# The Mamba stage of a kernel of eight sublayers: the input enters by a diagonal matmul, and GpSimd multiplies one half by C in every second step

## The chip, the cores and the metric

One core of one Trainium2 chip runs the kernel. The metric is the device time of one execution in microseconds (us). Times below without another unit are us from the start of the profiled span. VectorE is DVE in the profile, ScalarE is ACT, GpSimd is POOL, TensorE is PE (PEld its weight loads), and the queue of the transfers is SP.

## The reference

Eight sublayers follow one another on x of shape 4 x 1024 x 128 in float32. The change touches only the fifth, a Mamba block with 256 inner channels and 16 states:

```python
xs, z = jnp.split(xn @ W_in.T, 2, axis=-1)
u = jax.nn.silu(conv(xs))                      # depthwise, 4 taps
dt_low, Bc, Cc = jnp.split(u @ W_xproj.T, [DT_RANK, DT_RANK + D_STATE], axis=-1)
delta = jax.nn.softplus(dt_low @ W_dt.T + b_dt)
def step(h, inp):                              # over the 1024 tokens
    dt, bt, ct, ut = inp
    h = jnp.exp(dt[..., None] * A) * h + (dt * ut)[..., None] * bt[:, None, :]
    return h, jnp.einsum('bdn,bn->bd', h, ct)
y = (ys + u * D_param) * jax.nn.silu(z)
return resid + y @ W_out.T
```

## The kernel before

The Mamba stage works in 64 **steps** N, one for each batch b (4) and state n (16): N = 16 b + n. In a step the recurrence over 1024 tokens is one `tensor_tensor_scan` for each half c of the 256 channels: 128 channels lie on the partitions, the tokens along the free dimension. For a step the engines do the following.

- ScalarE, `decay` (L1671): exp(delta * A) of 128x1024 for both halves into `da`. `scale_input` (L1683): eight activations, one for each block of 128 tokens, multiply the block of delta * u (`duT`, tokens on partitions, 256 channels) by the column of B of this state. The result, eight tiles of 128x256, goes to `scaled`, double buffered in the tiles that were called rope, causal and toeplitz.
- TensorE, `drive` (L1544): eight transposes for each half bring `scaled` into PSUM banks 0 to 3 (two banks for each half), channels on partitions. A half's banks are free when its scan of the step before has ended.
- VectorE (L1776): scan of half 0, scan of half 1. Then at most one piece of the layer norm of a later batch, and (L1790) the product of `h` and the row of C, in place, for half 0 and for half 1.
- GpSimd (L1836): for each half, `y_sum` += product. The scan of step N + 2 writes the same buffer of `h` and so waits for this addition of step N.
- SP (L1808): loads the row of C, spread over 128 partitions (512 KB), two buffers. It waits for the products of step N - 2.

Beside the steps of batch b the input of batch q = b + 1 is prepared, one part behind each step, in an order that is written out by hand. TensorE: `convolve` in n = 0, 1, 3, 4; `low_rank` in 5; `gate_input` 0 in 6; `delta` in 7 and 8; `gate_input` 1 in 9; `rates_to_tokens` (B, L1501) in 10; `input_to_tokens` in 12 and 13. All of them use PSUM banks 6 and 7, so that each waits until the part before it is read. ScalarE: `take_convolved` in 2, 3, 5, 6; `activate` (Silu) in 6; `take_low` and `direct` 0 in 7; `take_gate` 0 (Silu, L1641) and `direct` 1 in 8; `take_delta` (L1647, L1649) in 9 and 10; `soften` (Exp, then Ln, L1654 and L1656) in 10; `take_gate` 1 in 11. Silu, Exp and Ln each need a table load of their own when ScalarE changes to them. VectorE copies B from PSUM in step 12 (`take_rates`, L1760); GpSimd computes delta and delta * u in steps 10 and 11 (`step_size`, L1819 and L1822). In steps 2 and 3 the batch before is finished (`results`, L1532).

For batch 0 the same parts run ahead of the first step, on TensorE in the order low, delta, `rates_to_tokens`, gates, `input_to_tokens`. There VectorE copies B only behind the norm of batch 1 (L905) and the last combination of the experts (L768).

Of the kernel before, what the change touches and what calls it, by code (L numbers as in the profile page):

```python
# [1424 lines left out]
def sp_load_stacks(nc, k, sp, sm, b):  # L1425

    for stack, tile in ((k.q_dram[b], k.q_stack[b % 2]), (k.k_dram[b], k.k_stack[b % 2])):
# [5 lines left out]
          "drive", "scan", "prod", "y_sum", "gated", "y_ps", "x_new"]  # L1433
# [12 lines left out]


def pe_mamba(nc, k, pe, sm, moe):

    bank_reader = [None, None]  # L1450

    def take_banks(*halves):
        for g in halves:
            if bank_reader[g]:
                pe.wait_ge(sm[bank_reader[g][0]], bank_reader[g][1])

    def tokens(q):
        take_banks(0, 1)
        for t in range(8):
            if t % 4 == 0:  # L1460
                pe.wait_ge(sm["xn2"], 2 * q + t // 4 + 1)
            mm = nc.tensor.transpose(k.ps[:, PREP + t // 4, (t % 4) * P:(t % 4 + 1) * P], k.XN2s[:, t, :], k.ident[:])
            if t % 4 == 3:
                mm.then_inc(sm["xnT_ps"], 1)
        bank_reader[:] = [("xnT", 2 * q + 1), ("xnT", 2 * q + 2)]

    def convolve(q, c, g):
        take_banks(g)
# [27 lines left out]
    def rates_to_tokens(q):
        take_banks(0)
# [6 lines left out]
        bank_reader[0] = ("bT", q + 1)  # L1504

    def delta(q, c):
        take_banks(0, 1)
        pe.wait_ge(sm["low"], q + 1)
        for g in range(2):
            mm = nc.tensor.matmul(k.ps[:, PREP + g, :], k.WdtT[96:112, c * P:(c + 1) * P], half(k.low[q % 2][96:112, :], g),  # L1510
                                  start=True, stop=True)
        mm.then_inc(sm["delta_ps"], 1)
        bank_reader[:] = [("relu", 2 * q + c + 1)] * 2

    def input_to_tokens(q, r):
        take_banks(0, 1)
        pe.wait_ge(sm["du"], 2 * q + 2)
        for t in range(4 * r, 4 * r + 4):
            g = t % 4 // 2
            for c in range(2):  # L1520
                mm = nc.tensor.transpose(k.ps[:, PREP + g, (t % 2) * 256 + c * P:(t % 2) * 256 + (c + 1) * P],
                                         k.soft[:, c, t * P:(t + 1) * P], k.ident[:])
            if t % 2 == 1:
                mm.then_inc(sm["duT_ps"], 1)
                bank_reader[g] = ("duT", 4 * q + 2 * r + g + 1)

    def results(b):
        take_banks(0, 1)
# [1201 lines left out]
```

## Time and profile before

| what | value |
|---|---|
| three executions | 3139.59, 3144.19, 3144.25 us |
| median of them | 3144.19 us |
| the profiled execution | 3142.85 us, of it the span 3141.1 us |
| first scan, end of the last product | 1901.8 and 2403.9 us: 64 steps in 502.1 us |
| single ScalarE instructions: one half of `decay`; `take_low`; `direct`; one gate; one of `take_delta`'s two; one of `soften`'s two; a table load | 1.14; 1.00; 1.14; 1.02; 1.10; 1.91; 1.28 us |
| the four batches of 16 steps | 132.0, 133.7, 126.6 and 109.8 us |

The profiled execution lies between the runs that were timed and 1.3 us below their median. A row of the timeline gives start, duration, engine, line and operation, and in brackets the idle time of the engine before it and what ended it; neighbours of one kind are merged ("x2"), and the duration is then that of all of them.

### The profile page before, as it was taken

How to read it: one execution, taken by the hardware profiler on the slowest of the kernel's cores; microseconds unless marked ns; L12 is line 12 of the kernel's file. 1: busy time of each engine (PE TensorE's matmuls, PEld its weight loads, DVE VectorE, ACT ScalarE, POOL GpSimd, SP SyncE). 2: the span in 40 equal slices, each digit the busy share in tenths (PEclk: the TensorE clock that was granted, in tenths of full speed). 3: DMA queues.
4: the chain of work that ended last, by engine and by line, in shares of the span. 5: the costliest groups of instructions: out<-in, count | busy, mean ns of one | idle time of the engine just before them, and what ended most of it. 6: DMA issues, size and time to landing. Idle time of an engine off the chain costs nothing.

```text
span 3141.1 us, 55341 instructions
## 1 busy us (share of the span) xinstructions
PE 2592.3 (83%) x19200; PEld 1636.5 (52%) x19200; DVE 2033.0 (65%) x4702; ACT 1779.8 (57%) x3375; POOL 910.1 (29%) x995
## 2 busy tenths in 40 slices
PE   7999799989988998688994856676655988888878
PEld 4667466756665666574444834445443622322325
DVE  5654565456645564557866447898897877777745
ACT  4665466556655665251111438988984446666662
POOL 1000000000000000673005765767776122322221
PEclk9999899989999999699996978677756979999999
DMA  5000000000000000130001311121121530110000
GB/s 178 1 0 1 2 1 0 1 2 1 0 2 1 1 0 25 48 89 20 1 0 36 89 52 47 62 67 62 68 74 63 200 105 2 56 55 2 2 2 28
DMA packets 79895, 113.47 MB, mean 36 GB/s; under 512 B 10109, under 2 KB 48172, under 8 KB 79680
## 3 DMA queue, kind: packets, MB, share of 16 engines
q1 hardware_dynamic: 71488, 97.07, 9.4%
q0 software_dynamic: 8192, 13.67, 1.6%
q8 instruction: 118, 1.93, 0.3%
q14 instruction: 97, 0.79, 0.1%
HBM read 77.66 MB, written 35.78 MB: 36 GB/s over the span
## 4 chain that ended last, share of the span: by engine, by line
PE 21%; POOL 16%; issue 14%; DVE 9%; ACT 1%; POOLq 0%; DVEq 0%; SPq 0%; ACTq 0%
POOL arena L1836 6%; DVE Wqkv L2107 5%; POOL arena L829 4%; PE ps L1983 4%; PE ps L991 3%; POOL slots_in L815 3%; PE ps L1156 3%; PE ps L1955 2%; PE ps L1944 1%; PE ps L1165 1%; PE ps L982 1%; PE ps L1948 1%; PE ps L1992 1%; DVE X L768 1%; PE ps L1191 0%
## 5 line engine op out<-in xcount | busy, mean ns | idle before, releaser
L356 ACT ACTIVATE arena<-ps 128x512 f32<-128x512 f32 (+1 forms) x640 | 334.3, 548 | 309.1 <-PE ps L260 307.7
L432 DVE CUSTOM_DVE_ANT_0 arena<-ps,causal 128x512 f32<-128x512 f32 (+3 forms) x512 | 282.5, 589 | 328.5 <-PE ps L247 328.2
L369 ACT ACTIVATE arena<-arena 128x640 f32<-128x640 f32 (+7 forms) x512 | 394.1, 770 | 36.2 <-DVE arena L432 32.4
L2107 DVE TENSOR_REDUCE Wqkv<-ps 128x2 f32<-128x1024 f32 (+3 forms) x384 | 353.4, 953 | 87.0 <-PE ps L1948 81.7
L2063 ACT ACTIVATE arena<-ps 128x1024 f32<-128x1024 f32 (+3 forms) x384 | 302.4, 809 | 162.3 <-PE ps L1955 158.7
L260 PE MATMUL ps<-ident,arena 128*128 128x128 f32 x2304 | 346.2, 282 | 46.6 <-ACT arena L369 44.6
L1836 POOL TENSOR_TENSOR arena<-arena,W 128x1024 f32<-128x1024 f32 x128 | 333.6, 2626 | 170.4 <-DVE W L1790 170.4
L509 POOL COPY arena<-arena 128x512 f32<-128x512 f32 x64 | 39.5, 617 | 1040.0 <-DVE arena L456 621.4
L260 PEld LDWEIGHTS ps<-ident,arena 128*128 128x128 f32 x2304 | 250.6, 141 | 165.4 <-issue 139.6
L281 PE MATMUL ps<-arena,rope 128*64 128x128 f32 x4608 | 336.3, 281 | 0.0
L1776 DVE TENSOR_TENSOR_SCAN W<-arena,ps 128x1024 f32<-128x1024 f32 x128 | 285.2, 2269 | 56.0 <-ACT arena L1671 45.5
L281 PEld LDWEIGHTS ps<-arena,rope 128*64 128x64 f32 x4608 | 243.6, 136 | 64.3 <-issue 53.5
L247 PE MATMUL ps<-arena 64*128 64x512 bf16 (+3 forms) x2304 | 232.2, 325 | 5.1 <-ACT rope L348 5.1
L1983 PE MATMUL ps<-arena,W 128*32 128x512 f32 (+3 forms) x1536 | 164.4, 500 | 7.2 <-POOL arena L2134 3.6
L1955 PE MATMUL ps<-arena 64*128 64x512 bf16 (+3 forms) x768 | 124.6, 333 | 46.4 <-DVE Wqkv L2107 39.5
L1671 ACT ACTIVATE arena<-arena,A_neg 128x1024 f32<-128x1024 f32 x128 | 142.5, 1141 | 20.1 <-DVE W L1776 19.5
L1790 DVE TENSOR_TENSOR W<-W,select 128x1024 f32<-128x1024 f32 x128 | 153.1, 1237 | 0.5
L1944 PE MATMUL ps<-arena 64*128 64x512 bf16 (+3 forms) x768 | 133.3, 344 | 19.7 <-DVE Wqkv L2107 18.3
L2134 POOL TENSOR_SCALAR_AFFINE_SELECT arena<-arena 128x256 f32<-128x256 f32 x256 | 103.5, 408 | 158.1 <-ACT arena L2063 156.6
L1544 PE MATMUL ps<-ident,rope 128*128 128x128 f32 x512 | 99.0, 362 | 60.8 <-DVE W L1776 55.3
L198 PE MATMUL ps<-XNT,arena 128*128 128x512 f32 x256 | 137.8, 667 | 11.3 <-DVE arena L407 8.6
L247 PEld LDWEIGHTS ps<-arena 64*128 64x128 bf16 x2304 | 88.9, 94 | 109.5 <-issue 50.9
(262 smaller groups left out, 4608.7 us busy)
## 6 DMA issues: line engine op xcount, KB each, us to landing
select<-c_rows SPq DMA_DIRECT2D x64, 512.0 KB, 3.6
arena<-q_dram SPq DMA_DIRECT2D x4, 2048.0 KB, 9.6
arena<-k_dram SPq DMA_DIRECT2D x4, 2048.0 KB, 15.2
q_dram<-arena SPq DMA_DIRECT2D x24, 256.0 KB, 3.7
k_dram<-arena SPq DMA_DIRECT2D x24, 256.0 KB, 3.7
arena<-slots_in SPq DMA_DIRECT2D x8, 640.0 KB, 5.0
slots_out<-arena SPq DMA_DIRECT2D x8, 640.0 KB, 3.8
slots_in<-select SPq DMA_DIRECT2D x4, 640.0 KB, 6.3
```

Source lines behind the costliest of these rows:

```text
L247: mm = nc.tensor.matmul(k.ps[:, banks[h], 0:w], q, kk, start=part == 0, stop=part == 2)
L260: mm = nc.tensor.transpose(k.ps[:, 4 + m % 2, (b - b0) * P:(b - b0 + 1) * P], k.prob[:, n % 2, h, j * P:(j + 1) * P], k.ident[:])
L281: mm = nc.tensor.matmul(k.ps[64 * h:64 * h + 64, 6 + n // 4, (n % 4) * P:(n % 4 + 1) * P], k.v_tok[:, parity, j, 64 * h:64 * h + 64], k.pr ...
L356: nc.scalar.activation(k.probT[:, n % 2, b0 * P:(b0 + nb) * P], k.ps[:, 4 + m % 2, 0:nb * P], ACT.Copy)\
L369: nc.scalar.activation(k.prob[:, i % 2, h, 0:w], k.prob[:, i % 2, h, 0:w], ACT.Exp, bias=k.neg_max[:, i % 2, h:h + 1], scale=-1.0, accum_o ...
L432: ins = nc.vector.tensor_tensor_reduce(k.prob[:, i % 2, h, 512 * g:512 * g + w], k.ps[:, banks[h], 0:w], k.causal[:, first:first + w], 1.0 ...
L1776: nc.vector.tensor_tensor_scan(k.h[:, 2 * (n % 2) + c, :], k.da[:, 2 * (n % 2) + c, :], both(k.ps[:, 2 * c:2 * c + 2, :]), 0.0, ALU.mult, ...
L1836: nc.gpsimd.tensor_tensor(y, y, k.h[:, 2 * (n % 2) + c, :], ALU.add).then_inc(sm["y_sum"], 1)
L1955: mm = nc.tensor.matmul(k.ps[:, 2 * slot + h, 0:w], k.k_stack[b % 2][rows, 2 * Q + a, j * P:(j + 1) * P], k.q_stack[b % 2][rows, 2 * Q + a ...
L1983: mm = nc.tensor.matmul(k.ps[32 * r:32 * r + 32, 6, 512 - w:512], k.v_aug[b % 2][:, j, 4 * Q + r, :], k.expT[:, (2 * s + a) % 4, h, 0:w], ...
L2063: nc.scalar.activation(k.expT[:, n % 4, :, 0:w], k.ps[:, 2 * (m % 3):2 * (m % 3) + 2, 0:w], ACT.Exp, scale=-1.0)\
L2107: nc.vector.tensor_reduce(k.least[:, g, a, i % 4, c, :], k.ps[:, 2 * (m % 3):2 * (m % 3) + 2, 0:search_width(i, c)], AX_X, ALU.min)\
```

## The change

1. `scale_input` no longer scales the data. It multiplies the 128x128 identity by the column of B, eight activations of 128x128 instead of 128x256, into `diag` (two buffers, both in rope). `drive` multiplies: data block (128 tokens x 128 channels, from `duT`) times diagonal, 16 full float32 matmuls in a step in place of 16 transposes.
2. In every odd step the product with C of half 1 is computed on GpSimd, ahead of its two additions. The other three products of two steps stay on VectorE.
3. The preparation uses four PSUM banks (4 to 7), so that parts no longer wait for the reader of the part before; the order is new.
4. For batch 0 the copy of B has a bank of its own (bank 0).

```diff
@@ pe_mamba
-                mm = nc.tensor.matmul(k.ps[:, PREP, t * NSTATE:(t + 1) * NSTATE], k.u[:, c, t * P:(t + 1) * P],
+                mm = nc.tensor.matmul(k.ps[:, at, t * NSTATE:(t + 1) * NSTATE], k.u[:, c, t * P:(t + 1) * P],
...
     def drive(N, c):
+        b = N // NSTATE
         if c == 0:
+            if N % NSTATE == 0:
+                pe.wait_ge(sm["duT"], 4 * b + 4)
             pe.wait_ge(sm["scaled"], 2 * N + 2)
         if N >= 1:
             pe.wait_ge(sm["scan"], 2 * N - 1 + c)
         for t in range(8):
-            mm = nc.tensor.transpose(k.ps[:, 2 * c + t // 4, (t % 4) * P:(t % 4 + 1) * P],
-                                     k.scaled[N % 2][t // 4][:, t % 4, c * P:(c + 1) * P], k.ident[:])
+            mm = nc.tensor.matmul(k.ps[:, 2 * c + t // 4, (t % 4) * P:(t % 4 + 1) * P],
+                                  k.duT[:, 8 * (b % 2) + t, c * P:(c + 1) * P], k.diag[N % 2][:, t, :], start=True, stop=True)
...
-            if n == 5:
+            if n in (5, 6):
+                gate_input(q, n - 5)
+            if n == 7:
                 low_rank(q)
-            if n == 6:
-                gate_input(q, 0)
-            if n in (7, 8):
-                delta(q, n - 7)
-            if n == 9:
-                gate_input(q, 1)
+            if n in (8, 9):
+                delta(q, n - 8)
@@ act_mamba
-            ins = nc.scalar.activation(k.scaled[N % 2][t // 4][:, t % 4, :], k.duT[:, 8 * (b % 2) + t, :], ACT.Identity,
-                                       scale=k.bT[:, at:at + 1])
+            ins = nc.scalar.activation(k.diag[N % 2][:, t, :], k.ident[:], ACT.Identity, scale=k.bT[:, at:at + 1])
...
-            if n == 6:
+            if n == 7:
                 activate(q)
-            if n == 7:
+                take_gate(q, 0)
+                take_gate(q, 1)
+            if n == 8:
                 take_low(q)
                 direct(q, 0)
-            if n == 8:
-                take_gate(q, 0)
-                direct(q, 1)
...
             if n == 11:
-                take_gate(q, 1)
+                direct(q, 1)
@@ dve_mamba
-        for c in range(2):
+        for c in range(1 if shares_product(N) else 2):
             dve.wait_ge(sm["scan"], N * 2 + c + 1)
@@ sp_mamba
-            sp.wait_ge(sm["prod"], 2 * (N - 1))
+            sp.wait_ge(sm["prod"], products_by_dve(N - 2, 1))
+            if shares_product(N):
+                sp.wait_ge(sm["pool_prod"], N // 2)
@@ pool_mamba
+        if shares_product(N):
+            pool.wait_ge(sm["scan"], 2 * N + 2)
+            pool.wait_ge(sm["c_row%d" % (N % 2)], 16 * (N // 2 + 1))
+            h = k.h[:, 2 * (n % 2) + 1, :]
+            nc.gpsimd.tensor_tensor(h, h, k.c_rows[N % 2], ALU.mult).then_inc(sm["pool_prod"], 1)
```

The new helpers: `shares_product(N)` is `N % 2 == 1`; `products_by_dve(N, c)` counts VectorE's products up to step N; `gate_bank(w)` gives bank 6 or 4; `rates_bank(q)` gives bank 0 for batch 0 and 4 for the others. The wait for the last readers of the experts' banks (`yt_act`, `yt_dve`) moves from ahead of the first `drive` to ahead of `rates_to_tokens(0)`.

## Rows read from the trace of the kernel before

**Rows 1.** The page: busy time by engine over the whole span.

```profile
PE 2592.3 (83%) x19200; PEld 1636.5 (52%) x19200; DVE 2033.0 (65%) x4702; ACT 1779.8 (57%) x3375; POOL 910.1 (29%) x995
```

**Rows 2.** Windows per batch: width; PE, PEld, DVE, ACT, POOL busy; clock, DMA share, GB/s.

```profile
1901.80:2033.80 132.00, 86.65 (x378) 61.36 (x377) 119.72 (x117) 123.05 (x202) 95.99 (x37) 0.77 0.18 61
2033.80:2167.50 133.70, 94.95 (x401) 67.05 (x400) 122.18 (x121) 117.22 (x191) 91.04 (x39) 0.72 0.19 64
2167.50:2294.10 126.60, 87.27 (x400) 61.92 (x398) 112.91 (x71) 117.83 (x191) 96.62 (x37) 0.80 0.19 67
2294.10:2403.90 109.80, 57.11 (x272) 46.89 (x272) 109.61 (x69) 76.87 (x140) 78.61 (x33) 0.62 0.21 72
```

**Rows 3.** Waits between 1900 and 2400 us: total, times, longest.

```profile
...
DVE W L1776 <- ACT arena L1671: 45.5, 7, 19.3
...
DVE W L1776 <- issue: 10.5, 6, 3.0
...
```

**Rows 4.** Groups by line and shape, ScalarE: busy us, mean ns of one, idle before.

```profile
L369 ACT ACTIVATE arena<-arena 128x128 f32<-128x128 f32 x64 | 25.7, 401 | 4.1 <-DVE arena L432 4.1
```

**Rows 5.** Timeline before the first scan.

```profile
1882.19 0.29 DVE L1760 COPY arena<-ps 128x128 f32<-128x128 f32 x1
1882.54 3.42 PE L1481 MATMUL ps<-arena,WinT 128*128 128x512 f32 x4 [22.23 <-DVE arena L1760]
...
1895.99 3.30 ACT L1683 ACTIVATE rope<-arena 128x256 f32<-128x256 f32 x8
...
1901.79 4.46 DVE L1776 TENSOR_TENSOR_SCAN W<-arena,ps 128x1024 f32<-128x1024 f32 x2 [19.31 <-ACT arena L1671]
```

**Rows 6.** Timeline of VectorE and of GpSimd, one step of the last batch.

```profile
2383.96 4.45 DVE L1776 TENSOR_TENSOR_SCAN W<-arena,ps 128x1024 f32<-128x1024 f32 x2
2388.34 2.33 DVE L1790 TENSOR_TENSOR W<-W,select 128x1024 f32<-128x1024 f32 x2
2390.59 2.27 DVE L1776 TENSOR_TENSOR_SCAN W<-arena,ps 128x1024 f32<-128x1024 f32 x1
...
2382.98 4.87 POOL L1836 TENSOR_TENSOR arena<-arena,W 128x1024 f32<-128x1024 f32 x2 [1.76 <-DVE W L1790]
2385.86 1.99 POOL L1836 TENSOR_TENSOR arena<-arena,W 128x1024 f32<-128x1024 f32 x1
```

**Rows 7.** Timeline of VectorE and of GpSimd, one step of the third batch.

```profile
2175.45 5.58 POOL L1836 TENSOR_TENSOR arena<-arena,W 128x1024 f32<-128x1024 f32 x2 [4.03 <-DVE W L1790]
...
2180.80 1.32 DVE L1790 TENSOR_TENSOR W<-W,select 128x1024 f32<-128x1024 f32 x1
```

**Rows 8.** Timeline where a product meets a GpSimd instruction.

```profile
2255.61 2.00 POOL L1822 TENSOR_TENSOR W<-arena,W 128x1024 f32<-128x1024 f32 x1
2255.89 2.79 DVE L1790 TENSOR_TENSOR W<-W,select 128x1024 f32<-128x1024 f32 x1
```

**Rows 9.** Timeline of TensorE: eight transposes; results twice (high, lower clock); low_rank.

```profile
2060.43 1.06 PE L1544 MATMUL ps<-ident,rope 128*128 128x128 f32 x8 [0.56 <-DVE W L1776]
...
2056.14 3.74 PE L1532 MATMUL ps<-WoutT,arena 128*128 128x128 f32 x32
...
1948.28 3.66 PE L1491 MATMUL ps<-W,WxT 128*112 128x512 f32 x8 [1.97 <-ACT W L1618]
...
2410.27 5.84 PE L1532 MATMUL ps<-WoutT,arena 128*128 128x128 f32 x32 [13.21 <-DVE arena L1747]
```

**Rows 10.** Timeline of ScalarE, TensorE and VectorE in steps 10 to 12.

```profile
1979.29 1.10 ACT L1647 ACTIVATE W<-ps,s_cols 128x1024 f32<-128x1024 f32 x1
...
1993.13 1.28 ACT L1641 ACT_TABLE_LOAD   x1
...
1988.91 4.46 DVE L1776 TENSOR_TENSOR_SCAN W<-arena,ps 128x1024 f32<-128x1024 f32 x2 [2.25 <-ACT arena L1671]
2004.39 4.46 DVE L1776 TENSOR_TENSOR_SCAN W<-arena,ps 128x1024 f32<-128x1024 f32 x2 [6.06 <-ACT arena L1671]
...
1995.50 4.66 PE L1501 MATMUL ps<-WxT,W 128*128 128x16 f32 x21 [9.94 <-ACT arena L1641]
```

More of the change, by code:

```diff
@@ L1432 @@
           "low_ps", "low", "c_stored", "c_row0", "c_row1", "bT_ps", "bT", "delta_ps", "abs", "relu", "soft", "delta", "du", "duT_ps", "duT", "scaled", "da",
-          "drive", "scan", "prod", "y_sum", "gated", "y_ps", "x_new"]
+          "drive", "scan", "prod", "pool_prod", "y_sum", "gated", "y_ps", "x_new"]
 NSTATE = 16
@@ L1440, in both, with shares_product, products_by_dve, gate_bank @@
     return ap.rearrange("p a b -> p (a b)")
+def shares_product(N):
+    return N % 2 == 1
+def products_by_dve(N, c):
+    return 3 * (N // 2) + (3 if shares_product(N) else c + 1)
 def state_steps(k):
     return [(b, n) for b in range(k.B) for n in range(NSTATE)]
+def gate_bank(w):
+    return (6, 4)[w]
+def rates_bank(q):
+    return 4 if q else 0
 def pe_mamba(nc, k, pe, sm, moe):
[L1450 to L1455, printed above, removed]
+    bank_reader = {bank: None for bank in (4, 5, 6, 7)}
+    def take_banks(*banks):
+        for bank in banks:
+            if bank_reader[bank]:
+                pe.wait_ge(sm[bank_reader[bank][0]], bank_reader[bank][1])
     def tokens(q):
-        take_banks(0, 1)
+        take_banks(6, 7)
         for t in range(8):
@@ L1461, in tokens @@
                 pe.wait_ge(sm["xn2"], 2 * q + t // 4 + 1)
-            mm = nc.tensor.transpose(k.ps[:, PREP + t // 4, (t % 4) * P:(t % 4 + 1) * P], k.XN2s[:, t, :], k.ident[:])
+            mm = nc.tensor.transpose(k.ps[:, 6 + t // 4, (t % 4) * P:(t % 4 + 1) * P], k.XN2s[:, t, :], k.ident[:])
             if t % 4 == 3:
                 mm.then_inc(sm["xnT_ps"], 1)
-        bank_reader[:] = [("xnT", 2 * q + 1), ("xnT", 2 * q + 2)]
+        bank_reader[6], bank_reader[7] = ("xnT", 2 * q + 1), ("xnT", 2 * q + 2)
     def convolve(q, c, g):
-        take_banks(g)
+        bank = 4 + 2 * c + g
+        take_banks(bank)
         if c == 0 and g == 0:
@@ L1490, in low_rank @@
             for g in range(2):
-                mm = nc.tensor.matmul(k.ps[0:112, PREP + g, :], k.WxT[:, c, 0:112], half(k.u[:, c, :], g), start=(c == 0),
+                mm = nc.tensor.matmul(k.ps[0:112, 6 + g, :], k.WxT[:, c, 0:112], half(k.u[:, c, :], g), start=(c == 0),
                                       stop=(c == 1))
         mm.then_inc(sm["low_ps"], 1)
-        bank_reader[:] = [("low", q + 1)] * 2
+        bank_reader[6] = bank_reader[7] = ("low", q + 1)
     def rates_to_tokens(q):
-        take_banks(0)
+        at = rates_bank(q)
+        if q >= 1:
+            take_banks(at)
         pe.wait_ge(sm["u"], q + 1)
@@ L1524, in input_to_tokens @@
                 mm.then_inc(sm["duT_ps"], 1)
-                bank_reader[g] = ("duT", 4 * q + 2 * r + g + 1)
+                bank_reader[bank] = ("duT", 4 * q + t // 2 + 1)
     def results(b):
-        take_banks(0, 1)
+        take_banks(6, 7)
         pe.wait_ge(sm["gated"], 2 * b + 2)
@@ L1640, in take_gate @@
             act.wait_ge(sm["y_ps"], 2 * (q - 1))
-        nc.scalar.activation(k.z[q % 2][:, w, :], both(k.ps[:, PREP:PREP + 2, :]), ACT.Silu).then_inc(sm["z"], 1)
+        at = gate_bank(w)
+        nc.scalar.activation(k.z[q % 2][:, w, :], both(k.ps[:, at:at + 2, :]), ACT.Silu).then_inc(sm["z"], 1)
     def take_delta(q, c):
@@ L1658, in take_input @@
     def take_input(q, r):
+        if q >= 2:
+            act.wait_ge(sm["drive"], 32 * (q - 1))
         for g in range(2):
@@ L1661, in take_input @@
             at = 8 * (q % 2) + 4 * r + 2 * g
-            nc.scalar.activation(both(k.duT[:, at:at + 2, :]), k.ps[:, PREP + g, :], ACT.Copy).then_inc(sm["duT"], 1)
+            nc.scalar.activation(both(k.duT[:, at:at + 2, :]), k.ps[:, 4 + 2 * r + g, :], ACT.Copy).then_inc(sm["duT"], 1)
     def decay(N):
@@ L1677, in scale_input @@
             act.wait_ge(sm["bT"], b + 1)
-            act.wait_ge(sm["duT"], 4 * b + 4)
         if N >= 2:
@@ L1828, in pool_mamba @@
     for N, (b, n) in enumerate(state_steps(k)):
+        if shares_product(N):
[3 more added lines that the diff above has]
+            nc.gpsimd.tensor_tensor(h, h, k.c_rows[N % 2], ALU.mult).then_inc(sm["pool_prod"], 1)
         for c in range(2):
-            pool.wait_ge(sm["prod"], 2 * N + c + 1)
+            if c == 1 and shares_product(N):
+                pool.wait_ge(sm["pool_prod"], N // 2 + 1)
+            else:
+                pool.wait_ge(sm["prod"], products_by_dve(N, c))
             if n == 0:
@@ L2360, in build @@
         k.taps = spare.take([4, 256])
-        k.scaled = [[k.rope[:, q, :].rearrange("p (t c) -> p t c", t=4) for q in range(2)],
-                    [k.causal[:].rearrange("p (t c) -> p t c", t=4), k.toeplitz[:, 0:1024].rearrange("p (t c) -> p t c", t=4)]]
+        k.diag = [k.rope[:, q, :].rearrange("p (t c) -> p t c", t=8) for q in range(2)]
         k.XN2s = k.Wo[:]
```

44 lines of the change are left out of this document (24 added, 20 removed).

## The prediction, made before the changed kernel was run

> **What bounds the kernel now.** The page comes first: TensorE is busy for 83% of the span [rows 1], but that is a mean over eight sublayers, and the change touches 502 us of them. The windows per batch say what holds the stage: VectorE is busy 119.7 of 132.0, 122.2 of 133.7, 112.9 of 126.6 and 109.6 of 109.8 us, while ScalarE has 117 to 123 in the first three and only 76.9 in the last, which prepares nothing [rows 2]. So VectorE is the bound of the last batch, and VectorE and ScalarE together of the others. The waits name what VectorE lacks: 45.5 us for ScalarE's `decay` and 10.5 for "issue", mostly TensorE's drive; 19.3 of the sum of 56.0 is the time before the first scan, which leaves 36.7 us inside the three batches with preparation [rows 3]. The timeline then gives the step: scans start at 2383.96, products at 2388.34, the next scans at 2390.59, so a step without anything else is 6.63 us, 4.38 of scans and 2.25 of products [rows 6].
>
> One more thing is to be seen there. GpSimd's first addition takes 2.88 us (4.87 for both, 1.99 for the second), and VectorE's second product lies over its beginning [rows 6]. The reverse stands in [rows 8]: a product that starts at 2255.89, while GpSimd is at work until 2257.61, takes 2.79 instead of the 1.20 that it takes alone. It therefore ran only from 2257.5. GpSimd's instruction and a product exclude each other; the scans, of which one input is in PSUM, run beside GpSimd unhindered. In the third batch an addition takes 2.35 and the pair 5.58: it ends at 2181.03, the product that began at 2180.80 takes 1.32, and so VectorE loses 0.12 in each step already (6.75) [rows 7].
>
> **Before the first scan.** Today B is copied at 1882.48, only then come gate, Silu and transposes, and the scaling at 1895.99; the scan is at 1901.79 [rows 5]. With a bank of their own the gates and `duT` are done while VectorE still combines the experts. Behind the copy remain: eight diagonals of 128x128. One 128x128 takes 0.40 [rows 4]; eight of 128x256 take 3.30 [rows 5], and by the difference of 0.09 between instruction length and pitch I take 2.5. Then eight matmuls: 16 of them take 3.74 at the high clock, 0.234 each [rows 9], thus twice that, 3.7, after the idle time. 1882.5 + 2.5 + 3.7 and 0.3 of handing over give 1889.0, and ScalarE's table load of 1.28 and decay of 1.1 lie beside it. **-12.8** (bounds -10 and -14: one more table load, or the high clock).
>
> **Stalls in the preparation, 36.7 us.** Of the two in batch 0 that ScalarE causes, 2.25 is in front of step 11 and 6.06 in front of step 12 [rows 10]. The first is a chain: `take_delta` 1 starts at 1979.29, soften with two loads and the decay follow, the scan starts at 1988.91, 9.6 later. The second: gate 1 between steps 11 and 12 needs Silu, so two loads of 1.28 and 1.0, and TensorE's `rates_to_tokens` stands 9.94 us behind this gate and holds up the drive of step 12 [rows 10]. The change puts both gates behind `activate`, under one table, and frees the banks: the second stall goes, and most of what "issue" shows. The first grows. `low_rank` now lies in n = 7, behind a drive that waits for step 7's second scan (4.4 + 1.9 after its start), and takes 3.7 [rows 9]: ScalarE reads it at about 3 us into step 8, then runs low 1.0, direct 1.1, decays 2.2 and diagonals 2.5, delta 2.1, decays, diagonals, and reaches `take_delta` 1 about 3 us into step 10, where today it is 0.7 ahead of it. 3 + 9.6 - 6.7 gives 6 us, plus half a microsecond: 6.5 in each batch, 19.5 in all. **-17** (bounds -37: ScalarE keeps its lead; 0: the lead is lost elsewhere). ScalarE's 0.8 us less in each step (3.30 to 2.5) is worth something only through this lead; the last batch gets nothing of it.
>
> **Products.** VectorE gives up 1.11 us in two steps; 13.26 would be 12.15. But GpSimd now has five instructions in these two steps, 5 x 1.96 + 0.9 for each product in its way. I follow the last batch from the first product of the even step (time 0): products until 2.3, scans from 2.25; additions 1.27 to 4.2 and to 6.1. At 6.63 VectorE begins its only product, until 7.83; GpSimd's product begins at 6.8, has to let it pass, and ends at 7.83 + 1.86 = 9.7 (today's first addition ends at 2385.89, 1.86 after the second product's 2384.03 [rows 6]); the additions end at 11.6 and 13.6. VectorE's next scans end at 12.15, and its product finds GpSimd's last addition in the way until 13.5. Two steps: 13.5 against 13.26, if GpSimd's product takes 2.0; 13.85 with 2.35. I take +0.35 for eight pairs: +3. In the third batch the same walk ends in a tie at 12.25 (which of the two gets in first): 14.0 +- 0.4 against 13.50, eight pairs: +4. In the first two batches norm pieces and stalls give GpSimd time to catch up, but where a piece lies in an odd step GpSimd's product slips in ahead of VectorE's: +2. **+9** (bounds: -35, 32 products at 1.11 and nobody in the way; +23, 14.36 in every pair of batches 0 and 2 and 13.85 in the others). On this point the Trainium skill, SBUF — State Buffer, section "SBUF: two separate sides", says that a VectorE instruction with two SBUF inputs and a GpSimd one that reads SBUF lock each other out for the whole instruction. The trace agrees except that the lock is free 0.12 us before the end that is recorded [rows 7, 8]; by whole instructions the sum would be about 2 us more.
>
> SP's row of C for an odd step now waits for GpSimd's product, about 3 us after the scans, where it was 2.3; the next odd step needs it 10 us later. Nothing. The end: behind the last scan come product 3.0 and two additions 4.0 instead of 1.2 and 4.9: **+1**.
>
> **TensorE.** Sixteen matmuls are 3.74 at the high clock, 7.5 at the low; eight transposes are 1.06 [rows 9], so the pair was 2.1. Drive 0 of the next step may start when scan 0 ends and has 4.4 us (even to odd) or 3.3 (odd to even, plus the 1.3 that VectorE waits anyhow): enough at the high clock, 0.4 to 1.9 late at the low. The granted clock is 0.72 to 0.80 in the first three batches and 0.62 in the last [rows 2]. I take late drives in about a third of the steps at 0.3: **+6** (bounds 0 and +33, below).
>
> **Sum.** 3142.85 - 12.8 - 17 + 9 + 1 + 6 = 3129.0 us. The profiled execution is 1.3 below the median of the three runs, so against 3144.2 this is 0.5% less.
>
> **Rivals.** A measurement of this kernel tells about 0.2%, 6 us, from nothing.
>
> *As summed*, 3113 to 3137: 0.42.
>
> *TensorE is raised to the high clock.* The last batch has only transposes on TensorE and the lowest clock, 0.62, though TensorE is busy for 57.1 of 109.8 us [rows 2]. If denser matmuls bring the high clock, the 6 us for late drives go and with them some 4 us of the chain through `low_rank` and `delta`: 3142.85 - 12.8 - 21 + 9 + 1 = 3119. Chance 0.12. The Trainium skill, TensorE: Matmul & The Clock Gate, section "Part 4: PE-mode transpose", says that transposes don't count as work for the clock as matmuls do; the row of 0.62 speaks for it in part, not wholly, since the low level alone would be 0.50.
>
> *VectorE keeps all it gives up*, -35 in place of +9: 3085. Needs products that GpSimd doesn't stop, against [rows 8]. 0.08.
>
> *TensorE becomes the bound (slower).* the clock stays low while the work grows. 16 drives are 60 us at the high clock; the preparation is 30 to 38 (busy time of the first three batches less that of the last [rows 2]), at a clock of 0.76 that is 26 at the high one. 86 us at a clock of 0.62 are 139 for a batch, against 129, 131 and 124 that my sum gives: +33 in place of +6, 3156. It decides below a clock of 0.67. 0.15.
>
> *GpSimd becomes the bound*: +23 in place of +9: 3143, on either side. For it: 96 of 132 us busy before [rows 2], plus 8 x 2.35 and what is blocked. Against it: the stalls that remain give GpSimd time. 0.14.
>
> *The stall stays*: `low_rank`, later by a step, costs all that the gates give: -17 goes, 3146. 0.09.
>
> Together faster by over 0.2%: 0.42 + 0.12 + 0.08 and a third of the last two, 0.69; within 0.2%: 0.09; slower 0.22. The range reaches from half way to 3085 up to the TensorE case: 3102 to 3157; the likeliest case alone has 3113 to 3137.
>
> **What would show it.** First scan at 1889 instead of 1901.8. No wait over 1 us in front of steps 12, one of about 6 in front of steps 11. VectorE's products: maximum near 3 us and a mean above 1.4 instead of 1.2; GpSimd's first product instruction near 2.9. In the last batch two steps in 13.5 to 13.9, so the batch at 112 to 115 against 109.8. "Issue" or TensorE ahead of scans under 8 us in all. I am wrong if the last batch gets shorter (no exclusion), if TensorE is named ahead of most scans, or if the wait before steps 11 is gone or doubled.

## The result and the profile after

The changed kernel takes 3137.35 us in the median of 15 runs, the kernel before 3143.0 us in 15 runs beside them: a ratio of 0.9981 (95% interval 0.9973 to 0.9989), 0.19% less. Forecast were 3129.0 us, 0.48% less. The time lies in the range that was given (3102 to 3157) and just above that of the likeliest case (3113 to 3137). The direction held, the size of the gain did not: 5.7 us of the medians, where some 14 were forecast.

The profiled execution takes 3134.85 us, 8.0 less than that of before. The timeline of the changed kernel around its first scan:

```profile
1880.15 0.29 DVE L1786 COPY arena<-ps 128x128 f32<-128x128 f32 x1
...
1880.47 2.44 ACT L1711 ACTIVATE rope<-ident,arena 128x128 f32<-128x128 f32 x8 [7.29 <-DVE arena L1786]
...
1883.06 5.86 PE L1571 MATMUL ps<-rope,arena 128*128 128x128 f32 x32 [10.51 <-ACT rope L1711]
...
1886.92 4.47 DVE L1802 TENSOR_TENSOR_SCAN W<-arena,ps 128x1024 f32<-128x1024 f32 x2 [6.48 <-PE ps L1571]
```

Between the end of the copy of B and the first scan lie 6.5 us; before they were 19.3 [rows 5]. The copy itself comes 2.0 earlier, as everything ahead of it does; nothing that the change touches lies there.

Groups of VectorE and GpSimd in the stage of the changed kernel (busy us, mean ns of one, idle time before and its cause; of the eight products with the gate, L1773, two lie behind the stage, and inside it their wait is 4.2 us):

```profile
L1802 DVE TENSOR_TENSOR_SCAN W<-arena,ps 128x1024 f32<-128x1024 f32 x128 | 285.5, 2268 | 26.2 <-ACT arena L1700 18.1 <-PE ps L1571 7.7 <-issue 0.4
L1816 DVE TENSOR_TENSOR W<-W,select 128x1024 f32<-128x1024 f32 x96 | 150.3, 1591 | 0.5
L905 DVE TENSOR_SCALAR Wo<-XN,mv,rstd 128x128 f32<-128x128 f32 x16 | 16.2, 1070 | 0.0
L1773 DVE TENSOR_TENSOR arena<-arena 128x1024 f32<-128x1024 f32 x8 | 9.4, 1223 | 10.4 <-POOL arena L1872 10.4
L905 DVE TENSOR_SCALAR XN<-X,mv,rstd 128x128 f32<-128x128 f32 x16 | 9.1, 632 | 0.0
L898 DVE TENSOR_SCALAR var_eps<-mv 128x8 f32<-128x8 f32 x4 | 6.5, 1618 | 0.1
...
L1861 POOL TENSOR_TENSOR W<-W,select 128x1024 f32<-128x1024 f32 x32 | 92.3, 2885 | 10.0 <-DVE W L1802 10.0
```

The waits ahead of scans fell from 56.0 us [rows 3] to 26.2, and of these 6.5 are ahead of the first: 36.7 became 19.7. But 96 products take 150.3 us, about what 128 took before (153.1). One takes 1.59 instead of 1.24, so VectorE gave up 32 products and its products are busy for only 3 us less. The norm's scalar instructions (L905, L898) take 31.8 us where they were 13.3.

Two steps of the last batch, VectorE and then GpSimd:

```profile
2359.16 4.45 DVE L1802 TENSOR_TENSOR_SCAN W<-arena,ps 128x1024 f32<-128x1024 f32 x2
2363.53 1.19 DVE L1816 TENSOR_TENSOR W<-W,select 128x1024 f32<-128x1024 f32 x1
2365.20 4.46 DVE L1802 TENSOR_TENSOR_SCAN W<-arena,ps 128x1024 f32<-128x1024 f32 x2 [0.48 <-ACT arena L1700]
2369.59 3.49 DVE L1816 TENSOR_TENSOR W<-W,select 128x1024 f32<-128x1024 f32 x2
2372.99 2.27 DVE L1802 TENSOR_TENSOR_SCAN W<-arena,ps 128x1024 f32<-128x1024 f32 x1
...
2363.69 3.25 POOL L1861 TENSOR_TENSOR W<-W,select 128x1024 f32<-128x1024 f32 x1 [0.65 <-DVE W L1802]
2366.91 3.94 POOL L1872 TENSOR_TENSOR arena<-arena,W 128x1024 f32<-128x1024 f32 x2
2372.02 2.91 POOL L1872 TENSOR_TENSOR arena<-arena,W 128x1024 f32<-128x1024 f32 x1 [1.17 <-DVE W L1816]
```

The odd step has one product (2363.53) and would let VectorE run ahead. But GpSimd's product, started at 2363.69 and held up by VectorE's until 2364.7, ends at 2366.94, its two additions at 2370.85, and VectorE's pair of products from 2369.59 takes 3.49 instead of 2.33 [rows 6]: its first had to wait for the last addition. From 2359.16 to 2372.99 the two steps take 13.83 us; before it was 13.26.

In the third batch it is more. The scans that start at 2205.61 and 2220.28 are those of odd steps:

```profile
2202.31 3.38 DVE L1816 TENSOR_TENSOR W<-W,select 128x1024 f32<-128x1024 f32 x1
2205.61 4.45 DVE L1802 TENSOR_TENSOR_SCAN W<-arena,ps 128x1024 f32<-128x1024 f32 x2
2209.99 1.31 DVE L1816 TENSOR_TENSOR W<-W,select 128x1024 f32<-128x1024 f32 x1
2211.70 4.46 DVE L1802 TENSOR_TENSOR_SCAN W<-arena,ps 128x1024 f32<-128x1024 f32 x2 [0.41 <-issue]
2216.08 4.27 DVE L1816 TENSOR_TENSOR W<-W,select 128x1024 f32<-128x1024 f32 x2
2220.28 2.27 DVE L1802 TENSOR_TENSOR_SCAN W<-arena,ps 128x1024 f32<-128x1024 f32 x1
...
2201.26 8.95 POOL L1872 TENSOR_TENSOR arena<-arena,W 128x1024 f32<-128x1024 f32 x3
2210.17 3.34 POOL L1861 TENSOR_TENSOR W<-W,select 128x1024 f32<-128x1024 f32 x1
```

GpSimd works from 2201.26 to 2218.1 without a gap, and one product of VectorE takes 3.38. Two steps take 14.7 us (2205.61 to 2220.28), before 13.50. Five GpSimd instructions of 2.35 would be 11.8 us, so GpSimd's own work doesn't fill the two steps: it does so together with the time in which VectorE's products hold it up.

### The profile page after: what moved, and what is told of

Its sections match the earlier page's. It is cut to its first block, busy times and chain, and to the rows that moved or that the text cites. A ratio compares the mean times of both kernels' runs of the same rounds, so it can differ in the third digit from the quotient of the medians.

```text
span 3133.1 us, 57443 instructions
## 1 busy us (share of the span) xinstructions
PE 2656.1 (85%) x20224; PEld 1733.1 (55%) x20224; DVE 2048.8 (65%) x4670; ACT 1708.4 (55%) x3363; POOL 972.7 (31%) x1027
## 4 chain that ended last, share of the span: by engine, by line
PE 21%; POOL 17%; issue 14%; DVE 9%; ACT 1%; POOLq 0%; DVEq 0%; SPq 0%; ACTq 0%
POOL arena L1872 6%; DVE Wqkv L2143 5%; POOL arena L829 4%; PE ps L2019 4%; PE ps L991 3%; POOL slots_in L815 3%; PE ps L1156 3%; POOL W L1861 2%; PE ps L1991 2%; PE ps L1980 1%; PE ps L1165 1%; PE ps L982 1%; PE ps L1984 1%; PE ps L2028 1%; POOL arena L1847 1%
## 5 line engine op out<-in xcount | busy, mean ns | idle before, releaser
L1571 PE MATMUL ps<-rope,arena 128*128 128x128 f32 x2048 | 289.8, 306 | 110.5 <-DVE W L1802 75.0
L1571 PEld LDWEIGHTS ps<-rope,arena 128*128 128x128 f32 x2048 | 276.4, 219 | 139.1 <-issue 94.8
L1872 POOL TENSOR_TENSOR arena<-arena,W 128x1024 f32<-128x1024 f32 x128 | 304.2, 2397 | 88.8 <-DVE W L1816 88.8
L1802 DVE TENSOR_TENSOR_SCAN W<-arena,ps 128x1024 f32<-128x1024 f32 x128 | 285.5, 2268 | 26.2 <-ACT arena L1700 18.1
L247 PE MATMUL ps<-arena 64*128 64x512 bf16 (+3 forms) x2304 | 233.3, 327 | 5.1 <-ACT rope L348 5.1
L1711 ACT ACTIVATE rope<-ident,arena 128x128 f32<-128x128 f32 x512 | 156.2, 389 | 48.0 <-PE ps L1571 40.7
L1991 PE MATMUL ps<-arena 64*128 64x512 bf16 (+3 forms) x768 | 124.9, 334 | 46.6 <-DVE Wqkv L2143 39.8
L1700 ACT ACTIVATE arena<-arena,A_neg 128x1024 f32<-128x1024 f32 x128 | 141.8, 1141 | 36.8 <-DVE W L1802 36.7
L1816 DVE TENSOR_TENSOR W<-W,select 128x1024 f32<-128x1024 f32 x96 | 150.3, 1591 | 0.5
```

Source lines behind the costliest of these rows:

```text
L247: mm = nc.tensor.matmul(k.ps[:, banks[h], 0:w], q, kk, start=part == 0, stop=part == 2)
L1571: mm = nc.tensor.matmul(k.ps[:, 2 * c + t // 4, (t % 4) * P:(t % 4 + 1) * P], k.duT[:, 8 * (b % 2) + t, c * P:(c + 1) * P], k.diag[N % 2][ ...
L1802: nc.vector.tensor_tensor_scan(k.h[:, 2 * (n % 2) + c, :], k.da[:, 2 * (n % 2) + c, :], both(k.ps[:, 2 * c:2 * c + 2, :]), 0.0, ALU.mult, ...
L1872: nc.gpsimd.tensor_tensor(y, y, k.h[:, 2 * (n % 2) + c, :], ALU.add).then_inc(sm["y_sum"], 1)
```

## The experiments

They ran on three other chips, on which the kernel before takes 3257 to 3267 us, 3.6 to 4% more than on the chip of the result above (called the first chip). Nearly all of it lies ahead of the Mamba stage; inside the stage the steps take the same time (e4 against the kernel before, and e10, the changed kernel again, against its first run). So whole times are compared as ratios to the kernel before on the same chip, and the stage by its own length. In the table this runs from the first scan of the stage to the start of the last one, as the view of the scan's line gives it. Where an expectation speaks of the stage it counts 4.5 us more, from the start of the last scan to the end of the last product in the kernel before. The last batch of every row holds the same 4.5 us, also where GpSimd forms the last product and ends later.

| kernel | ratio (95%) | first to last scan | batches |
|---|---|---|---|
| before (first chip) | 1 | 497.6 | 132.0, 133.8, 126.5, 109.8 |
| changed (first chip) | 0.9981 (0.9973 to 0.9989) | 502.1 | 131.3, 132.5, 127.8, 115.0 |
| e1 no share | 0.9937 (0.9924 to 0.9951) | 484.5 | 128.1, 129.7, 121.2, 109.9 |
| e2 share only | 1.0035 (1.002 to 1.005) | 507.2 | 133.3, 133.2, 129.5, 115.7 |
| e3 transposes | 0.9947 (0.9931 to 0.9963) | 484.0 | 129.1, 128.4, 121.1, 109.9 |
| e4 early gates | 0.9995 (0.9981 to 1.0009) | 497.9 | 132.1, 133.9, 126.6, 109.9 |
| e5 left out | 0.9879 (0.9856 to 0.9902) | 459.6 | 120.0, 122.8, 116.9, 104.4 |
| e6 write only | 0.9919 (0.9893 to 0.9945) | 473.7 | 124.2, 126.2, 120.3, 107.4 |
| e7 share beside stats | 0.9983 (0.9969 to 0.9997) | 498.1 | 127.7, 132.2, 127.4, 115.3 |
| e8 low_rank early | 0.9984 (0.9969 to 0.9999) | 494.9 | 130.8, 134.0, 124.5, 110.2 |
| e9 share every step | 1.0105 (1.0079 to 1.013) | 530.9 | 138.6, 141.8, 134.4, 120.6 |
| e10 changed again | 1.0013 (1.0 to 1.0025) | 502.5 | 131.4, 133.2, 127.4, 115.0 |
| e11 no share again | 0.9954 (0.9935 to 0.9973) | 483.2 | 127.6, 129.9, 120.3, 109.8 |

**e1_no_share and e11_no_share_again.** The share undone, all else of the change kept:

```diff
 def shares_product(N):
-    return N % 2 == 1
+    return False
```

> The changed kernel with all products on VectorE again (the share undone, the rest kept). Theory A, exclusion: in the changed kernel VectorE's 96 products took 150.3 us (1.59 each, maximum near 3) where 96 x 1.20 is 115, and the norm's instructions on L905 and L898 took 31.8 us against 13.3 before; gates waited 4 us more inside the stage and 2.3 at its end. So the share costs about 35 + 18.5 + 6.3 - 32 x 1.11 = 24 us net, of which some hides in stalls: 3137 - 20 = 3117 (3112 to 3123), products at a mean of 1.24. Theory B, TensorE's full matmuls hold the stage and the share is neutral or helps: 3137 to 3170.

> All products on VectorE, the rest of the change kept, as e1_no_share, beside the changed kernel on one chip. Ratio 0.9937 to the kernel before, 13 to 18 us under the changed kernel, stage 489.

> The changed kernel itself, on the same chip as the next one. Ratio to the kernel before as measured, 0.998, stage 506 to 508.

Measured: e1 is 19.7 us under the kernel before, and its stage is 17.6 shorter than the changed kernel's (20 were expected). On one chip e11 is 18.3 us under e10 (3252.87 against 3271.2), and the stages are 483.2 and 502.5. Theory A holds, and this version beats both kernels. The ratio of e10 is not the 0.998 expected but 1.0013: on this chip the changed kernel has no gain (e4 below says why), while its stage is as expected. The groups of e1, for comparison with those of the changed kernel:

```profile
L1807 DVE TENSOR_TENSOR_SCAN W<-arena,ps 128x1024 f32<-128x1024 f32 x128 | 285.3, 2269 | 39.8 <-PE ps L1576 21.4 <-ACT arena L1705 18.0 <-issue 0.3
L1821 DVE TENSOR_TENSOR W<-W,select 128x1024 f32<-128x1024 f32 x128 | 155.2, 1253 | 0.5
...
L905 DVE TENSOR_SCALAR Wo<-XN,mv,rstd 128x128 f32<-128x128 f32 x16 | 11.5, 783 | 0.0
...
L905 DVE TENSOR_SCALAR XN<-X,mv,rstd 128x128 f32<-128x128 f32 x16 | 4.8, 364 | 0.0
...
L898 DVE TENSOR_SCALAR var_eps<-mv 128x8 f32<-128x8 f32 x4 | 0.7, 172 | 0.1
```

From these rows to those of the changed kernel: products -4.9, the norm's scalar instructions +14.8 (17.0 to 31.8), gates waiting for GpSimd inside the stage +3.8 (0.4 to 4.2), scans waiting +1.3 (18.4 to 19.7). That is 15.0 of the 17.6 us. The rest is a matter of counting: records of neighbouring instructions overlap by some 0.08 us. Counted from the start of each VectorE instruction to the start of the next, products are at -2.9 (148.1 to 145.2), the norm at +14.8, the gates' waits at +3.8, scans and the waits ahead of them at +1.8, together 17.5.

**e2_share_only.** The kernel before with the share alone (the same edits of VectorE's, SP's and GpSimd's loops as in the change).

> The kernel before with the share alone (transposes, two PSUM banks and the old order kept). Theory A: the exclusion costs the same 20 us less what falls into stalls of the preparation, 36.7 us long here: 3143 + 15 = 3158 (3150 to 3165). Theory B: VectorE gets its 1.11 us back in 32 steps where ScalarE does not hold it: 3120 to 3143.

12.4 us slower than before (15 expected, 7 to 22), the stage 9.6 longer, the last batch 115.7 against 109.8. That is theory A.

**e3_transposes.** As e1, but scaled data and transposes as before:

```diff
-            mm = nc.tensor.matmul(k.ps[:, 2 * c + t // 4, (t % 4) * P:(t % 4 + 1) * P],
-                                  k.duT[:, 8 * (b % 2) + t, c * P:(c + 1) * P], k.diag[N % 2][:, t, :], start=True, stop=True)
+            mm = nc.tensor.transpose(k.ps[:, 2 * c + t // 4, (t % 4) * P:(t % 4 + 1) * P],
+                                     k.scaled[N % 2][t // 4][:, t % 4, c * P:(c + 1) * P], k.ident[:])
```

> As e1_no_share, but the input is scaled and transposed as before; order of the preparation, four banks and the early gates stay. Tells what the diagonal matmul alone is worth. Theory A: the diagonal is worth what ScalarE's lead is worth (0.86 us in each step) and the high clock: this is slower than e1_no_share by 3 to 12 us, 3120 to 3130, with a clock near 0.62 in the last batch. Theory B: full matmuls cost more than they give, so this one is faster than e1_no_share.

The time is 3.0 us above e1, the lower end of theory A, but the two intervals overlap, and the stage is equal (484.0 and 484.5). Neither theory is borne out: the diagonal matmul is worth nothing inside the stage and costs nothing there. The last batch of e1 and of e3 in windows (the columns as in [rows 2]):

```profile
2392.70:2502.60 109.90, 70.15 (x522) 65.61 (x521) 109.72 (x69) 64.78 (x140) 78.60 (x33) 0.92 0.21 72
```

```profile
2395.40:2505.30 109.90, 59.25 (x272) 49.16 (x272) 109.69 (x69) 76.92 (x140) 78.76 (x33) 0.59 0.20 72
```

ScalarE is spared 12 us and the clock goes from 0.59 to 0.92, and VectorE, busy for 109.7 of 109.9 us in both, is not moved.

**e4_early_gates.** The kernel before with bank 0 for B of batch 0 and the wait for the experts' banks moved:

```diff
-        take_banks(0)
+        at = PREP if q else 0
+        if q:
+            take_banks(0)
...
-    pe.wait_ge(moe["yt_act"], 2 * k.B)
-    pe.wait_ge(moe["yt_dve"], k.B)
     drive(0, 0)
```

> The kernel before with only the bank of its own for B of batch 0 (bank 0) and the wait for the experts' banks moved with it. First scan at about 6 to 8 us behind the copy of B instead of 19.3: 8 diagonal-less scalings 3.3, transposes 2 to 3.5, so -12: 3131 (3128 to 3134). Rival: the time is given back at the next wait of the preparation: 3143.

A miss: 3.0 us less in the medians, 0.05% by the ratio, with an interval that holds zero. The stage is as long as before (497.9), so the rival is wrong too: nothing was given back in it. The gain isn't there from the start, since on this chip the preparation of batch 0 is late itself. Batch 0 in e4:

```profile
1998.46 0.29 DVE L1763 COPY arena<-ps 128x128 f32<-128x128 f32 x1 [3.34 <-PE ps L1503]
...
2000.16 2.34 POOL L1822 TENSOR_TENSOR arena<-arena,W 128x1024 f32<-128x1024 f32 x1 [17.36 <-ACT W L1659]
...
2007.31 2.35 POOL L1825 TENSOR_TENSOR W<-arena,W 128x1024 f32<-128x1024 f32 x1
...
2014.32 3.30 ACT L1686 ACTIVATE rope<-arena 128x256 f32<-128x256 f32 x8
```

And e2, which has the old order, on the same chip:

```profile
1976.88 0.69 ACT L1622 ACTIVATE W<-ps,conv_w 128x512 f32<-128x512 f32 x1 [10.54 <-remote]
...
1980.93 6.31 PE L1500 MATMUL ps<-W,WxT 128*112 128x512 f32 x8 [20.38 <-ACT W L1627]
...
2005.65 2.34 POOL L1830 TENSOR_TENSOR arena<-arena,W 128x1024 f32<-128x1024 f32 x1 [23.96 <-ACT W L1665]
2006.23 0.29 DVE L1769 COPY arena<-ps 128x128 f32<-128x128 f32 x1 [12.23 <-PE ps L1510]
```

In e2 VectorE has finished the experts' combination at 1994 and waits 12.23 us for B; in e4 it still waits 3.34. GpSimd's delta and delta * u run from 2005.65 to 2015 in e2 and from 2000.16 to 2009.66 in e4, and behind them come the transposes that the first scan needs whatever the order of the gates. In both, and in e10 and e1 as well, the first scan starts 10.4 to 11.0 us behind the end of this GpSimd work (2026.2 and 2020.1 in e2 and e4). On the first chip it had ended at 1868.8 in the changed kernel, 11 us ahead of the copy of B. In the changed kernel on such a chip (e10) the first scan waits 19.69 us for TensorE; on the first chip it was 6.48. That fits the ratio of e10, 1.0013, against 0.9981: the one part that gained 12.8 us on the first chip has no gain clear of noise there. What the early gates alone are worth on the first chip was not run; the 12.8 us are read from its two timelines.

**e5_left_out.** The product of half 1 in odd steps is formed by nobody.

```diff
-            nc.gpsimd.tensor_tensor(h, h, k.c_rows[N % 2], ALU.mult).then_inc(sm["pool_prod"], 1)
...
-                pool.wait_ge(sm["pool_prod"], N // 2 + 1)
+                pool.wait_ge(sm["scan"], 2 * N + 2)
```

> The changed kernel with the product of half 1 in odd steps left out altogether: neither VectorE nor GpSimd forms it, the addition takes h as it is. Shows what VectorE's giving up 32 products is worth without any GpSimd work in its place. Stage (first scan to the end of the last) 506.6 in the changed kernel, 489 with no share. Exclusion: two steps of the last batch go to 12.2 us (VectorE's scans and three products, nobody in the way), the last batch to about 102 against 115, the stage to 460 to 470, and VectorE's products back to a mean under 1.3. If the product itself was never the matter (TensorE or ScalarE hold the steps), the last batch stays above 108.

**e6_write_only.** In its place GpSimd writes a dead buffer for as long as the product takes; the product is left out.

```diff
-            nc.gpsimd.tensor_tensor(h, h, k.c_rows[N % 2], ALU.mult).then_inc(sm["pool_prod"], 1)
+            nc.gpsimd.memset(k.toeplitz[:, 0:1920], 0.0)
+            nc.gpsimd.memset(k.causal[:, 0:512], 0.0).then_inc(sm["pool_prod"], 1)
```

> The changed kernel with GpSimd's product replaced by two memsets into a dead buffer, about 2.1 us together, as long as the product alone (2.0 to 2.35): the product is left out, GpSimd is as busy, but this part of its work reads nothing. If products and GpSimd exclude each other over reading, the memset no longer stops VectorE's product of the odd step nor is stopped by it; only additions that come 2.1 later still collide: last batch 105 to 109, stage 480 to 492. If it is plainly GpSimd's time (GpSimd the bound, no exclusion): last batch 113 to 115, stage 500 to 507.

The last batch is 104.4 in e5 (102 expected), 107.4 in e6 (105 to 109), 115.0 with the product; the stages with the 4.5 us are 464.1 (460 to 470 expected), 478.2 (480 to 492) and 506.6. So eight times 2.2 us of GpSimd work that reads nothing cost the last batch 3.0 us over none, and eight instructions of about that length that read cost 10.6. From e6's last batch, a product that starts during a memset, and then two steps, VectorE and GpSimd:

```profile
2408.53 1.70 POOL L1859 MEMSET toeplitz<- 128x1920 f32 x1 [0.62 <-DVE W L1802]
2409.56 1.22 DVE L1816 TENSOR_TENSOR W<-W,select 128x1024 f32<-128x1024 f32 x1
...
2455.60 4.45 DVE L1802 TENSOR_TENSOR_SCAN W<-arena,ps 128x1024 f32<-128x1024 f32 x2
2459.98 1.19 DVE L1816 TENSOR_TENSOR W<-W,select 128x1024 f32<-128x1024 f32 x1
2461.09 4.45 DVE L1802 TENSOR_TENSOR_SCAN W<-arena,ps 128x1024 f32<-128x1024 f32 x2
2465.47 2.94 DVE L1816 TENSOR_TENSOR W<-W,select 128x1024 f32<-128x1024 f32 x2
2468.33 2.27 DVE L1802 TENSOR_TENSOR_SCAN W<-arena,ps 128x1024 f32<-128x1024 f32 x1
...
2460.11 1.70 POOL L1859 MEMSET toeplitz<- 128x1920 f32 x1 [0.62 <-DVE W L1802]
2461.75 0.53 POOL L1860 MEMSET causal<- 128x512 f32 x1
2462.24 3.96 POOL L1871 TENSOR_TENSOR arena<-arena,W 128x1024 f32<-128x1024 f32 x2
```

The memset at 2460.11 begins 0.13 us after VectorE's product and is not held up by it (1.70, which is the median of all 32; the product takes 1.19); GpSimd's product in the same place took 3.25. Nor does a memset hold up a product: that at 2409.56 begins in the middle of one and takes 1.22. What remains in e6 is the collision of the last addition (to 2466.2) with the pair of products (2.94 instead of 2.33). The exclusion of a product of two SBUF tiles and a GpSimd instruction that reads SBUF is shown, and GpSimd's time alone is not the cause in this batch. Nor is it in the third: 116.9 in e5, 120.3 in e6, 127.8 with the product.

**e7_share_beside_stats.** VectorE forms both products in the steps where the norm's scalar instructions stand:

```diff
-    return N % 2 == 1
+    return N % 2 == 1 and (N >= 32 or N % 16 not in (3, 5, 9, 11))
```

> The changed kernel with VectorE forming both products in steps n = 3, 5, 9 and 11 of batches 0 and 1, the odd steps in which the norm's scalar instructions (L905, L898) stand between scan and product. If they are stopped by GpSimd's product: L905 and L898 in the stage fall from 31.8 us to 15 to 20, VectorE takes 8 x 1.11 more of products, and batches 0 and 1 together fall by 5 to 12 us from 263.8. If the norm is not the matter, batches 0 and 1 stay or grow by up to 9.

L905 and L898 fall to 17.4 us (11.9 + 4.8 + 0.7), as with no share (17.0): their excess was GpSimd's product in front of them. Batches 0 and 1 together fall by 3.9 us (259.9 against 263.8), less than the 5 to 12 expected, but not the stay or growth of the other theory. Batches 2 and 3, unchanged in this kernel, stay (127.4, 115.3).

**e8_low_rank_early.** As e1, with `activate`, the gates and `low_rank` one step earlier:

```diff
-            if n == 7:
+            if n == 6:
                 low_rank(q)
...
-            if n == 7:
+            if n == 6:
                 activate(q)
```

> All products on VectorE (as e1_no_share), and activate, the gates and low_rank one step earlier (n = 6). If the 18 us of waits ahead of steps 11 come from ScalarE reading low_rank late in step 8, each falls by about 3 us: the stage from 489 to 476 to 482, a ratio to the kernel before of 0.990 to 0.992 against 0.9937. Rival: TensorE now stands longer for u and delays the drives of steps 7 and 8, stage 487 to 495.

A miss, on the side of the rival and beyond its range: the stage is 10.4 us longer than e1's, 499.4 with the 4.5 us where the rival had 487 to 495. Waits ahead of scans for ScalarE rise from 18.0 to 26.8, in six places instead of three. Ahead of steps 11 they fall a little (18.0 to 13.9 in all), but 13.0 are new ahead of steps 7: ScalarE now stands 22.1 us, six times, for the gates' matmuls of TensorE, where in e1 it stands 8.6, three times.

**e9_share_every_step.** The suspect doubled:

```diff
-    return N % 2 == 1
+    return True
```

> The changed kernel with GpSimd forming the product of half 1 in every step, the suspect doubled. By the exclusion, walked as for two steps: last batch, GpSimd product until 3.05, additions until 5.0 and 7.0, VectorE's next product in at 6.85, a step of 6.85 and a batch of 113 to 115; batches 0 and 2, where one instruction is 2.35, are GpSimd's own time, 3 x 2.35 + 0.9 = 7.95 a step, 131 to 134. Stage 510 to 525 against 506.6. If giving VectorE's work away were good and something else spoiled the changed kernel, this one would be at 490 to 500.

Slower than before by 1.05%, and longer than expected wherever a range was given: the last batch 120.6 instead of 113 to 115, batches 0 and 2 138.6 and 134.4 instead of 131 to 134, the stage 535.4 instead of 510 to 525. For the last batch the expectation took 2.0 for GpSimd's product, of which none of the 64 is under 2.34. VectorE's 64 products take 141.8 us, 2.2 each. The direction is that of the exclusion, and the more is given to GpSimd, the longer it gets.

## Why the prediction was right and wrong

Its terms against what the first chip shows (the stage's parts by e1 on another chip, where the stage keeps its length):

| term | forecast | measured |
|---|---|---|
| ahead of the first scan | -12.8 | -12.8 (19.3 to 6.5 us behind the copy of B) |
| stalls in the preparation | -17 | -13.1 with the late drives (497.6 to 484.5, e1) |
| products | +9 | +17.6 (484.5 to 502.1) |
| late drives | +6 | in the row of the stalls; scans waited 1.2 us for TensorE in the changed kernel |
| behind the last scan | +1 | +2.4 |
| ahead of the stage, not by the change | 0 | -2.0 |
| sum, profiled execution | -13.8 | -7.9 |

The sum came out 5.9 us too low: +8.6 by the products, +1.4 behind the last scan, against -2.1 for stalls and late drives together (-11 forecast) and -2.0 ahead of the stage. The last is not of the change; without it the profiled gain is 5.9, and the medians have 5.7.

Most of what was to be seen in the profile came: VectorE's products at a mean of 1.59 (above 1.4 forecast) and at most 3.38 (near 3), GpSimd's at a mean of 2.89 (near 2.9), the last batch at 115.0, the upper end of 112 to 115, and the first scan 6.5 us behind the copy of B, as summed (1886.9 for 1889, because the copy came 2.0 earlier). Not so the waits: ahead of steps 11 they are 4.4, 3.6 and 4.3 (about 6 forecast), one step 12 has 1.4 (none over 1), and TensorE and "issue" have 8.1 in all (under 8).

**The step that failed is the size of the products' term**, "+9", which measures +17.6. The mechanism, that GpSimd's reading instructions and VectorE's products exclude each other, was right and is now shown by e5 and e6. What was mis-sized, batch by batch (e1 to the changed kernel):

- In the last batch GpSimd's product takes 2.35, not 2.0 (3.25 with VectorE's product in its way). The walk had 13.85 for two steps with it, measured are 13.83; I took a value between the two, and the term says +3 where the last batch has +5.1.
- In the third batch the walk gave 14.0 +- 0.4 and was left at a tie. Measured are 14.7, more than the 14.36 of the rival in which GpSimd becomes the bound; that rival came true in this batch. It grows by 6.6 instead of 4.
- "In the first two batches norm pieces and stalls give GpSimd time to catch up ... +2" is the sentence that is wrong in kind. The two grow by 3.2 and 2.8, 6.0 in place of 2. The pieces do not give time, they are stopped themselves: `tensor_scalar` on L905 and L898 waits for GpSimd's product. Counted from start to start, these instructions take 7.8 and 6.9 us more in the two batches, while the products take 3.3 and 4.0 less. e7, which takes GpSimd's product away from in front of them, brings them back to 17.4 us. I priced the pieces as something that lets GpSimd's product in first, and not as work that the exclusion holds up. The timeline of the changed kernel has it in one place; the norm's small instruction needs 0.17 alone:

```profile
1961.20 2.36 POOL L1861 TENSOR_TENSOR W<-W,select 128x1024 f32<-128x1024 f32 x1
...
1961.64 1.94 DVE L898 TENSOR_SCALAR var_eps<-mv 128x8 f32<-128x8 f32 x1
1963.49 1.21 DVE L1816 TENSOR_TENSOR W<-W,select 128x1024 f32<-128x1024 f32 x1
```

**The stalls** were right in place and size where the term can be read alone, without the share: in e1 VectorE waits 6.4, 5.3 and 6.3 us ahead of steps 11, 18.4 in all, where three waits of 6.5 were forecast. That the changed kernel has 19.7 where the forecast had 19.5 is luck: its three waits are 12.3, and the rest are small ones, many in the last batch, where none were forecast. The stage of e1 is only 13.1 shorter with 18.3 us less waiting, because other work grows: L905 takes 16.3 us in it where it took 12.6, the products 155.2 for 153.1. e3, with the transposes and a stage of 484.0, shows that all of this belongs to the order and the four banks, none to the diagonal.

**TensorE** did not become the bound. The condition of the rival in which matmuls raise the clock was met, but not its price: the clock is 0.87 to 0.91 in the four batches, against 0.62 to 0.80 [rows 2]. Inside the stage scans waited 1.2 us for TensorE and 0.4 for "issue", so the 6 us for late drives were for nothing. The Trainium skill, TensorE: Matmul & The Clock Gate, section "Part 4: PE-mode transpose", says that transposes don't count as work for the clock as matmuls do. e1 against e3 agrees in direction: 0.92 and 0.59 in a batch of equal length, with TensorE busy for 70.2 and 59.3 us of it. It does not agree that they don't count at all: this stretch of e3's last batch (the columns as in [rows 2]) has transposes alone on TensorE, at 0.61, between the two levels of 0.5 and 1:

```profile
2440.00:2500.00 60.00, 33.29 (x144) 26.89 (x144) 60.00 (x37) 42.78 (x78) 44.20 (x19) 0.61 0.22 79
```

The time that I put on this case did not follow, for almost nothing in the stage waited for TensorE.

**VectorE keeping all it gives up** is excluded by e1 against the changed kernel: the share costs 17.6 us. Even its price of 35 was too high. e5 takes 24.9 us off e1 when nobody forms the products: from start to start VectorE's products fall by 34.1 there, but scans wait 9.7 more, most of it for ScalarE's `decay`. So 24.9 is what the share would have been worth with a free GpSimd.

## What to carry to other kernels

Work moved from VectorE to GpSimd is not priced by GpSimd's idle time, but by what both of them do at once that reads SBUF: look in the trace for a VectorE instruction that started during a GpSimd one and took longer than alone, and count every instruction behind it of that sort, small scalar ones of a norm too. A scan with one input in PSUM ran beside GpSimd freely; a product of two SBUF tiles did not. And of a change with several parts, run it with each part undone: of the two that this change is named for, the diagonal was worth nothing and the share cost 17.6 us, more than the 13.1 that the reordering had gained.

## What the runs showed of the hardware that was not expected

- A GpSimd memset of 128x1920 ran beside a VectorE product with neither held up (1.70 and 1.19 us), where a GpSimd product in the same place took 3.25. But the norm's scalar instructions were held up by the memsets too: L905 and L898 take 28.1 us in e6 (14.7 + 8.5 + 4.9), 17.0 in e1. So these two kinds of VectorE instruction exclude different things. A third kind excludes nothing here: the norm's `BATCH_NORM_STATS2` (L892) takes 0.27 us in the changed kernel and in e1. The Trainium skill, SBUF — State Buffer, section "Who interferes with whom", draws this line: an instruction with two SBUF inputs collides with GpSimd's reads alone, one in a two-port mode with any use of the shared pair. The numbers agree, if these `tensor_scalar` run in a two-port mode, which no run here shows by itself.
- GpSimd's additions of one shape, where nothing holds them up, take 2.35 in batches 0 and 2 and 2.0 in batches 1 and 3; the buffer of `y_sum` alternates in the same way. Its product takes at least 2.35 in every batch (minimum 2354 ns of 32). What decides it was not tried.
- The chips of the experiments take 3.6 to 4% longer for the same kernel, nearly all of it ahead of this stage: the first scan of the changed kernel is at 2017.7 in e10 and at 1886.9 on the first chip, and of these 131 us 63 arise between 1330 and 1385 and 62 between 1740 and 1796, where GpSimd issues indirect transfers (L815, L829). Why they differ stays open. A part worth 12.8 us on the one has no gain clear of noise there (e4).
